# Products that nothing reads, in two places of TensorE's program in a two-layer block on one core

## What is computed

```python
Q = _l2norm(heads(Wq)); K = _l2norm(heads(Wk)); V = heads(Wv)
cos_sim = jnp.clip(jnp.einsum('bhtd,bhsd->bhts', Q, K), -0.999, 0.999)
scores = 1.0 - jnp.arccos(cos_sim) / jnp.pi
W = jnp.power(jnp.maximum(scores, EPS), POW)
W = W / (jnp.sum(W, axis=-1, keepdims=True) + EPS)
out = jnp.einsum('bhts,bhsd->bhtd', W, V).transpose(0, 2, 1, 3).reshape(B, T, D_OUT)
return jnp.einsum('bto,po->btp', out, Wo) + bo
...
x = x + _L0_attn_ref(xn, ...) + _L0_ffn_ref(xn, ...)
xn = _layernorm(x, axis=-1)
x = x + _L1_attn_ref(xn, ...) + _L1_ffn_ref(xn, ...)
```

## Time and profile before

| | before |
|---|---|
| time, median of 3 runs (lowest to highest) | 1970.91 us (1962.58 to 1976.08) |
| time of the profiled execution | 1969.34 us |
| its span, first to last instruction | 1967.5 us |
| PE busy | 1486.0 us, 76% |
| DVE busy | 1766.3 us, 90% |
| ACT busy | 1765.2 us, 90% |
| POOL busy | 1182.2 us, 60% |
| mean granted TensorE clock | 0.85 of full |

### The profile page before, as it was taken

One profiled execution on the slowest core, in us unless ns is written; L12 is line 12 of the kernel. 1 busy time (PEld: TensorE's weight loads), 2 busy tenths in 40 slices (PEclk: granted clock), 3 DMA queues, 4 the chain that ended last, 5 costly groups with the idle time before them and its releaser, 6 DMA issues.

```text
span 1967.5 us, 38505 instructions
## 1 busy us (share of the span) xinstructions
PE 1486.0 (76%) x12022; PEld 752.9 (38%) x12022; DVE 1766.3 (90%) x4009; ACT 1765.2 (90%) x1856; POOL 1182.2 (60%) x540
## 2 busy tenths in 40 slices
PE   2667787777777877777787787878777787777766
PEld 1223434333443433344343344343334434333433
DVE  5779999999999999999999999999999999999864
ACT  1299999999999999999999999899999999999893
POOL 1566666666666566566656666665667666665640
PEclk9578889889889888888978888897888889888776
DMA  1000000000000000000000000000000000000000
GB/s 42 3 4 1 6 1 6 5 6 6 6 3 3 6 5 6 6 6 0 6 6 5 6 5 6 0 6 6 5 6 5 6 0 6 6 5 6 4 3 6
DMA packets 21058, 11.19 MB, mean 6 GB/s; under 512 B 1431, under 2 KB 20953, under 8 KB 20956
## 3 DMA queue, kind: packets, MB, share of 16 engines
q1 hardware_dynamic: 20956, 10.20, 1.8%
HBM read 6.00 MB, written 4.19 MB: 5 GB/s over the span
## 4 chain that ended last, share of the span: by engine, by line
DVE 34%; ACT 24%; issue 22%; PE 16%; DVEq 1%; POOL 1%; SPq 0%; ACTq 0%; DMA 0%; POOLq 0%
ACT curve L578 13%; DVE nmax L880 6%; DVE curve L870 5%; ACT root L578 4%; PE psM L1037 3%; PE psM L1045 3%; DVE curve L874 3%; DVE acc L854 2%; PE psM L1190 1%; DVE stkT L866 1%; DVE xn L776 1%; ACT prob L578 1%; ACT L609 1%; PE psS L1095 1%; DVE h L454 1%
## 5 line engine op out<-in xcount | busy, mean ns | idle before, releaser
L530 POOL TENSOR_TENSOR root<-curve 128x2048 f32<-128x2048 f32 x128 | 478.7, 3740 | 453.1 <-DVE curve L874 453.1
L578 ACT ACTIVATE curve<-curve 128x2048 f32<-128x2048 f32 x384 | 718.8, 1907 | 5.5 <-POOL curve L533 2.2
L578 ACT ACTIVATE root<-root 128x2048 f32<-128x2048 f32 x256 | 484.6, 1906 | 0.0
L533 POOL TENSOR_TENSOR curve<-curve,root 128x2048 f32<-128x2048 f32 x64 | 354.5, 5562 | 64.4 <-ACT root L578 64.4
L578 ACT ACTIVATE prob<-psS 128x1024 f32<-128x1024 f32 x256 | 256.7, 1029 | 66.1 <-PE psS L1097 63.9
L874 DVE TENSOR_SCALAR curve<-psS 128x1024 f32<-128x1024 f32 x256 | 308.4, 1216 | 2.7 <-PE psS L1068 2.7
L880 DVE TENSOR_REDUCE nmax<-psS 128x4 f32<-128x1024 f32 x256 | 303.0, 1215 | 1.0 <-PE psS L1077 1.0
L566 POOL TENSOR_TENSOR stk<-qk,stk 128x512 f16<-128x512 f32 x128 | 147.8, 1164 | 76.9 <-ACT stk L578 76.6
L1045 PE MATMUL psM<-we,xnT 128*128 128x512 f32 x256 | 168.8, 747 | 0.0
L870 DVE TENSOR_TENSOR curve<-curve,root 128x2048 f32<-128x2048 f32 x64 | 162.0, 2531 | 6.1 <-ACT root L578 6.1
L1221 PE MATMUL psV<-curve,vc 128*32 128x256 f32 x2048 | 140.8, 406 | 29.8 <-ACT curve L578 25.9
(11 more groups left out here) (194 smaller groups left out, 2800.2 us busy)
## 6 DMA issues: line engine op xcount, KB each, us to landing
xt<-in_L_attn_x SPq DMA_DIRECT2D x32, 128.0 KB, 2.1
out<-yo SPq DMA_DIRECT2D x32, 128.0 KB, 1.8
we<-in_L_ffn_W_experts SPq DMA_DIRECT2D x1, 512.0 KB
curve<-in_L_attn_w_qkv SPq DMA_DIRECT2D x1, 192.0 KB
curve<-in_L_ffn_w_down SPq DMA_DIRECT2D x1, 176.0 KB
curve<-in_L_ffn_w_gate SPq DMA_DIRECT2D x2, 64.0 KB
curve<-in_L_ffn_w_up SPq DMA_DIRECT2D x2, 64.0 KB
curve<-in_L_ffn_W_qkv SPq DMA_DIRECT2D x1, 128.0 KB
```

The lines of the kernel that those rows point to most:

```text
L530: nc.gpsimd.tensor_tensor(root[:, two], curve[:, p, two], curve[:, p, two], ALU.mult).then_inc(s_sq, 1)
L533: nc.gpsimd.tensor_tensor(curve[:, p, two], curve[:, p, two], root[:, two], ALU.mult).then_inc(s_half[0], 1)
L578: return nc.scalar.activation(out, in_, func, **kw)
```

## The change

PE gets a helper that runs `count` matmuls of the identity with two experts' weights, 128 x 256 in f32, into PSUM that holds nothing at that time. It is called in two places: in `ocT` between the wait for the bank and the wait for `s_finc`, three products into the half of the bank that the transposes don't write; and behind the last unit of `m`, four products into the cosine attention's sums of `psV`, after a wait for ACT's copy of the batch whose sums stood there. Nothing reads them, and they raise no semaphore.

```diff
                     ins.then_inc(s_m, 1)
+                    if arg == UNITS - 1:
+                        pe.wait_ge(s_oC, due(s_oC, b - 2))
+                        keep_clock(psV[:, 0, 0, :], 4)
...
                     bank, k = misc_bank(stage, 0, 0)
                     last, value = bank_read(stage, 0, 0, t)
                     pe.wait_ge(last, value)
+                    keep_clock(bank[:, T:2 * T], 3)
                     pe.wait_ge(s_finc, due(s_finc, b))
                     for j in range(NT):
                         ins = transpose(bank[:, j * P:(j + 1) * P], oc[:, j, :], ident[:, :])
...
+            def keep_clock(spare_psum, count):
+
+                for k in range(count):
+                    mm(spare_psum, ident[:, :], we[:, 0:2, :].rearrange("p e f -> p (e f)"), start=True, stop=True)
```

## The result

The changed kernel takes 2003.53 us (median; 1994.41 to 2011.65), the kernel before beside it 1971.35: a ratio of 1.0167, 95% interval 1.0102 to 1.0232. It is slower, inside the range (1962 to 2027) and above the forecast of 1988, just outside the 1976 to 2002 that the prediction gave its forecast alone. The profiled execution took 2009.95 us, its span is 2008.2: 40.7 more than before.

A forecast was written before the change was run, and what follows sets the result against it. No engine alone was taken as the bound: a batch is one round through ACT, PE and DVE. To 1969.34 us came 14.4 for 28 steady batches and 4.6 outside them, giving 1988 us, range 1962 to 2027.

The forecast's parts named there:

- The first place does not fill the wait: At the cosine output's transposes: products also wait for the bank, so PE's 1.7 us of idling stay and products follow.
- The price, 1.6 us a batch: Three products ahead of the cosine output's transposes delay ACT and DVE by 1.6 us at high clock, 2.6 at low.
- The gain, at most 1.5 us: Fewer clock falls at the cosine output's transposes save at most 1.5 us per batch, none in the nine short ones.
- The second place at nothing: Four products before down: -0.2 to +1.2 us per batch, taken as 0 because the clock returns sooner.
- The sum: 22 batches at 58.1, six at 59.0: Steady batches: mean 58.3 us, 0.52 over 57.78, 14.4 us over 28; six still have a clock fall.
- The falls remain: Clock still falls before the transposes' products, which run at 1.2 GHz: 2026 us, if products average nearer 0.86 us; chance 0.18.
- The second place is late: Before down: clock returns no sooner, DVE's L943 stalls up to 1.2 us, 0.5 per batch left: 2002 us; chance 0.08.
- The price is swallowed: ACT or DVE makes good part of the 1.6 us as a later wait shrinks: 1969 us, no change; chance 0.08.
- The products do fill the waits: With the bank free before oc is done, products at its transposes cost nothing and falls go: 1936 us; chance 0.04.
- Low clock costs its half: Every low-clock stretch holds the batch up; half of 8.6 us returns in each of fourteen middle batches: 1909; chance 0.02.

The follow-up runs named there:

- e3_fill_first: Kernel before plus only the three products at the cosine output's transposes, placed ahead of the bank wait: 1978.26 us, ratio 1.0011.
- g2_first6_moved: Changed kernel with six products instead of three at the cosine output's transposes, none behind the row scores, third choose step (L839) earlier: 2041.37 us, ratio 1.0350.
- e2_second_only: Changed kernel without the three products at the cosine output's transposes; the four behind the last row scores stay: 1972.11 us, ratio 0.9991.
- e4_choose_moved: Changed kernel, all products kept, with VectorE's third choose step (L839) moved four places earlier: 1985.69 us, ratio 1.0054.
- its control: Kernel before, no products, with VectorE's third choose step (L839) moved earlier in the same way: 1975.52 us, ratio 1.0009.
- g3_fill_ocT_p1T: Kernel before plus three products ahead of the bank wait at the cosine output's transposes and two ahead of that at p1T: 1945.44 us, ratio 0.9872.

## Why the prediction was right, and where it was not

- **The first place does not fill the wait.** Right. The wait for `oc` ends at a product and is 1.5 us on average; with the products moved ahead of the bank wait (e3_fill_first) it is 0.6 us.
- **The price, 1.6 us a batch.** Right in kind, somewhat large: the transposes start 1.40 us behind the first product at the high clock, and up to 2.7 at the low one, where 2.6 was the bound. Three further ones cost 1.3 in the normal batches of g2_first6_moved. ACT and DVE wait for them in full (ACT's 1.90 us in the batch shown is just under the 2 foretold), and no steady batch is under 57.5 us, as foretold.
- **The gain, at most 1.5 us.** Right: middle batches of 58.0 stay at 57.8 to 58.3, short ones of 56.5 go to 57.8.
- **The second place at nothing.** Right for this kernel, and for the reason given: the clock returns before `down`, which makes good the 1.06 us. e2_second_only shows it by itself at 0.9991. But in a kernel whose other waits are filled the same four products cost 0.7%, by the clock further on and not by DVE's L943.
- **The sum: 22 batches at 58.1, six at 59.0.** This is the step that failed. Normal batches came out at 57.97, not 58.1, and the clock's falls left none at 59. Where the clock still falls, at the start of ten batches, it costs at most half a microsecond by itself (58.3 against 57.8) but takes L839's lead; four batches were 65 to 68 us long by a collision that the sum has no term for. The products' own price was sized too large (19 us in the sum, 9 by e4_choose_moved against its control), the collision of L839 and L533 was put at nothing and is some 22 us by the medians, 32 in the profiled execution. The two errors have opposite signs: that 2003.53 lies within the range is in part luck.
- **The rivals.** *The falls remain* gives 2026, 16 us over the profiled 2010, and its condition fails: a product took 0.47 us from start to start (1.40 for three) in 26 of 32 batches, not near 0.86. *The second place is late* gives 2002, the nearest figure of all, by a mechanism that the runs refute: DVE does not wait at L943, and e2_second_only stands at 0.9991. *The price is swallowed* fails too: at the high clock the batch is 1.3 us over the short ones' 56.5, for a price of 1.40. *The products do fill the waits* was priced at 1936 on the condition of a free bank. With that condition made true (e3_fill_first) nothing was gained; it took a second filled wait to get 1945. So its mechanism holds, but its step "the falls would go" was wrong as long as one is only pushed on. *Low clock costs its half* stays refuted: 0.99 at 58.25 us.
- **The collision could have been seen.** The trace of before has L839 0.46 to 0.64 us ahead of L533 in almost every batch, with nothing between them that would keep them apart, and in its last batch, which begins at the lower level, the lead is down to 0.16 us. The prediction asked who waits for a late PE, not whom a late DVE meets on POOL. The Trainium skill, page "SBUF — State Buffer", section "SBUF: two separate sides", says that a VectorE instruction with two inputs in SBUF contends with a GpSimd instruction that reads SBUF, that the one which starts first keeps the shared ports for its whole length and that the other is blocked. The rows here agree: L839 has two such inputs and 128 x 16 elements, and lasts to within 0.04 us of the end of a product 128 times its size. Only where L533 is 21 ns ahead or less by the trace is L839 not held.

What stays open: why a wait left unfilled at one place makes the clock fall at another, a batch's fifth away, isn't explained by the traces; they show where it falls, and that filling the next wait takes it away. Nor is it shown why the low clock comes to lie across the start of ten batches of the changed kernel.

## What to carry to other kernels

Work that is to keep TensorE's clock up has to stand ahead of every wait that it is to fill, the wait for its own PSUM bank among them; one instruction later it is paid in full by whoever reads what follows. Judge it by the length of the batches and by where the clock is low, not by the mean clock (0.917 was slower than 0.884), and expect a fall that is filled to turn up at the next wait before the gain comes. And when a change, or a low clock that it moves, delays VectorE by half a microsecond, look at which GpSimd instructions its small ones stand close to.

## What the runs showed of the hardware that was not expected

- A VectorE subtraction of 128 x 16 (0.16 us) takes 4.5 us when it starts 26 to 43 ns behind a GpSimd product of 128 x 2048 (all eight such starts in the profiles here), and 0.16 to 0.17 when it starts up to 21 ns behind it or at any time ahead of it; about 0.1 us behind a GpSimd subtraction of 128 x 512 it took 1.12.
- A fall of TensorE's clock can act by way of two other engines: a batch that began at 0.50 of the clock held VectorE up by 0.59 us, and of 270 batches the 29 that began so, and no others, had the subtraction within 0.2 us of that product.
- Filling one wait of 1.7 us left the time where it was (1.0011), and the low clock appeared in front of the projections, about 10 us earlier in the batch; filling that one too gave 1.3%. The same was seen a second time, with the second place (0.9942) and the experts' wait (0.9880).
- A batch of 57.78 us with the clock at 1.00 throughout (e4_choose_moved) is longer than one of 56.71 at 0.88 (g3_fill_ocT_p1T): 1.4 us of products on the path cost more than all the low clock that lies off it.
